# Last layer of a four-layer graph network: dots over halves of a turn, joined operations in the coefficients' chain, eight buffers of tails

## The reference

```
hyper_head = expmap0(head_emb)
hyper_tail = expmap(tail_emb, hyper_head)
hyper_rel = expmap(rel_emb, hyper_head)
res = project(mobius_add(hyper_tail, hyper_rel))
res = logmap(res, hyper_head) + ricci * 1e-07
res = jax.nn.relu(res)
sums = jnp.zeros((n_entities, res.shape[-1]), res.dtype).at[head].add(res)
...
return sums / jnp.clip(counts, 1.0, None)[:, None]
```

## Time and profile before

| | |
|---|---|
| time, median of 3 runs | 5223.61 us (5222.07 to 5224.58) |
| the profiled execution, first to last instruction | 6351.7 us |
| VectorE / GpSimd / TensorE / ScalarE busy in it | 3726.5 / 3463.1 / 2842.1 / 1728.7 us |
| mean granted TensorE clock | 0.618 |
| last layer in it | about 3205 us to the end |

### The profile page before, as it was taken

One profiled execution on the slowest core, in us unless ns is written; L12 is line 12 of the kernel. 1 busy time (PEld: TensorE's weight loads), 2 busy tenths in 40 slices (PEclk: granted clock), 3 DMA queues, 4 the chain that ended last, 5 costly groups with the idle time before them and its releaser, 6 DMA issues. The chain is left out here.

```text
span 6351.7 us, 75027 instructions
## 1 busy us (share of the span) xinstructions
PE 2842.1 (45%) x17919; PEld 2271.2 (36%) x17920; DVE 3726.5 (59%) x6870; ACT 1728.7 (27%) x5084; POOL 3463.1 (55%) x3375
## 2 busy tenths in 40 slices
PE   4544588433343334477614434434431343444442
PEld 1333456223333333345403333333331233333332
DVE  6444544255555666444426776667673767667678
ACT  0255200011111111000003354344340335445434
POOL 5667445466555663544265565566525556556551
PEclk7655699666666666678855555555555555555555
DMA  3720400355555554400021111111102111111110
GB/s 101 171 94 1 127 1 1 105 154 172 167 171 169 173 173 143 139 4 1 8 49 42 37 42 37 37 41 38 33 10 50 40 37 42 37 39 41 41 30 13
DMA packets 470914, 446.71 MB, mean 70 GB/s; under 512 B 113322, under 2 KB 417773, under 8 KB 470268
## 3 DMA queue, kind: packets, MB, share of 16 engines
q1 hardware_dynamic: 230602, 227.94, 12.4%
q0 software_dynamic: 116768, 136.51, 9.0%
q10 hardware_dynamic: 123282, 79.08, 4.5%
HBM read 306.93 MB, written 136.34 MB: 70 GB/s over the span
## 5 line engine op out<-in xcount | busy, mean ns | idle before, releaser
L2412 POOL DMA_INDIRECT tg<-tab_d,tail_ids x1632 | 1711.2, 1049 | 1191.1 <-DVEq L2731 644.9
L458 POOL DMA_INDIRECT sorted_edges_d<-place_batch x784 | 825.0, 1052 | 657.1 <-issue 220.6
L2437 PE MATMUL hr<-near_table,near_hot 128*128 x4896 | 654.4, 278 | 926.2 <-issue 593.1
L1598 POOL DMA_INDIRECT xg<-tab_d,src_i x784 | 768.0, 980 | 501.1 <-issue 241.6
L2445 PE MATMUL acc<-msg,sum_hot 128*96 128x65 f32 x3264 | 559.8, 364 | 902.1 <-ACT msg L2519 701.3
L2437 PEld LDWEIGHTS hr<-near_table,near_hot 128*128 128x128 f16 x4896 | 505.6, 108 | 1075.7 <-issue 970.2
L2445 PEld LDWEIGHTS acc<-msg,sum_hot 128*96 128x96 f32 x3264 | 536.4, 277 | 924.8 <-issue 924.7
L2492 ACT ACTIVATE pr<-hr 128x396 f32<-128x396 f32 x576 | 272.2, 482 | 1235.0 <-DMA b2col<-in_L_gnn_be_dram 786.9
L2513 ACT ACTIVATE pr<-pr,coef_c 128x64 f32<-128x64 f32 x1496 | 380.7, 340 | 82.4 <-issue 79.4
L2506 ACT ACTIVATE msg<-tg,coef_b 128x64 f32<-128x64 f32 x1632 | 399.1, 340 | 2.6 <-DVEq L2926 2.6
L2743 DVE TENSOR_REDUCE scal<-prod 128x17 f32<-128x1088 f32 x288 | 370.5, 1286 | 9.8
(11 more groups left out here) (504 smaller groups left out, 5392.9 us busy)
## 6 DMA issues: line engine op xcount, KB each, us to landing
ex<-spread_d SPq DMA_DIRECT2D x112, 448.0 KB
msg_d<-back ACTq DMA_DIRECT2D x112, 448.0 KB
near_hot<-head_row_d SPq DMA_DIRECT2D x96, 408.0 KB
tg<-tab_d,tail_ids POOLq DMA_INDIRECT x1632
spread_d<-zeros ACTq DMA_DIRECT2D x28, 896.0 KB
spread_d<-zeros SPq DMA_DIRECT2D x28, 896.0 KB
idsU<-dst_short_d SPq DMA_DIRECT2D x112, 224.0 KB
pairs_d<-pair_m SPq DMA_DIRECT2D x3, 4800.0 KB
```

The source lines that it names most:

```text
L458: l.eng.indirect_dma_start(K.sorted_edges[:, :], bass.IndirectOffsetOnAxis(ap=K.batch[:, n % 2, 0, k:k + 1], axis=0), K.batch[:, n % 2, 1, ...
L1598: l.eng.indirect_dma_start(xg[j.c % ROWS][:, half * H + k, :], None, K.tab1, bass.IndirectOffsetOnAxis(ap=src_i[:, t:t + 1], axis=0)).then ...
L2412: e.indirect_dma_start(tg[:, u % TAILS * GQ + k, :], None, K.tab3, bass.IndirectOffsetOnAxis(ap=K.tail_ids[:, u * GQ + k:u * GQ + k + 1], ...
L2437: ins = e.matmul(hr[(u * FILLS + g) % 2][:, c:c + PW3], near_hot[u % HOTS][:, k, :], rows[:, bass.ds(at[k] + n * PW3, PW3)], start=n == 0, ...
```

## The change

- `dot` works on halves of a turn: one product and one sum over 34 tiles (2176 elements per partition) for two over 17 each. It waits for both quarters of tails ahead of the product. `prod`, two tiles of a quarter, becomes one tile of two quarters.
- `TAILS` is 8, so that the tails of a turn lie next to each other (`T_`).
- In the chain, operations that stood side by side on neighbouring or evenly spaced rows of `sc` become one operation on two, three or four rows, partly with a broadcast. Rows are renumbered for it, and `kB`, `kC` become one tile `coef_bc`.
- Ten copies of lengths become three; the third, `PP`, is a packed copy of `PP_` (squared length of the head, read from `pr` with a stride), which the chain then reads.

```diff
-TAILS = 9
+TAILS = 8
...
-    prod = two("prod3", [P, GQ, D], F32)
+    prod = sb("prod3", [P, 2 * GQ, D], F32)
...
-            tt0(x[0], B, pt, MUL)
-            tt0(x[1], C, pr, MUL)
-            tt0(x[2], A, PP_, MUL)
+            tt0(terms[:, 0:3, :], abc, heads, MUL)
             tt0(x[3], C, tr, MUL)
-            tt0(x[4], B, q2[:, 0, :], MUL)
-            tt_(x[5], C, C, MUL)
+            tt_(terms[:, 4:6, :], abc[:, 1:3, :], q2, MUL)
...
-            def dot(n, x, y, quarters, taken=False, landed=False):
-                for q in quarters:
-                    u = now + q
+            def dot(n, x, y, halves, taken=False, landed=False):
+                for h in halves:
+                    at = slice(2 * h * GQ, (2 * h + 2) * GQ)
+                    u = now + 2 * h + 1
                     if taken:
                         v.wait_ge(near_taken, (u + 1) * FILLS)
                     if landed:
-                        v.wait_ge(got[u % TAILS], 16 * GQ * (u // TAILS + 1))
+                        for w in (u - 1, u):
+                            v.wait_ge(got[w % TAILS], 16 * GQ * (w // TAILS + 1))
                     v.wait_ge(l.sem, l.done())
-                    tt_(prod[q % 2][:, :, :], x(q), y(q), MUL)
+                    tt_(prod[:, :, :], x[:, at, 0:D], y[:, at, 0:D], MUL)
                     v.wait_ge(l.sem, l.done())
-                    v.tensor_reduce(sc[:, n, q * GQ:(q + 1) * GQ], prod[q % 2][:, :, :], AX.X, ADD).then_inc(l.sem, l.add(1))
-                    if q % 2 == 1:
-                        mark()
+                    v.tensor_reduce(sc[:, n, at], prod[:, :, :], AX.X, ADD).then_inc(l.sem, l.add(1))
+                    mark()
...
-            v.tensor_copy(q2[:, 1, :], R_[:, :, D])
-            for q in range(QN):
-                at = slice(q * GQ, (q + 1) * GQ)
-                v.tensor_copy(q2[:, 0, at], tg[:, tails(now + q), D])
-                v.tensor_copy(n2[:, 0, at], tg[:, tails(now + q), D + 1])
-            v.tensor_copy(n2[:, 1, :], R_[:, :, D + 1])
+            both_of = lambda x: x.rearrange("p k c -> p c k")
+            v.tensor_copy(sc[:, 2:25:22, :], both_of(T_[:, :, D:D + 2]))
+            v.tensor_copy(sc[:, 3:26:22, :], both_of(R_[:, :, D:D + 2]))
+            v.tensor_copy(PP, PP_)
...
-            for c in (cA, cB, cC):
-                tt_(c, c, A1(17), MUL)
+            tt_(abc, abc, three(A1(17)), MUL)
```

More of the change, by code:

```diff
@@ L2347, in edge_loop3 @@
     cA, cB, cC = (sc[:, n, :] for n in (26, 27, 28))
-    kB, kC = (two(n, [P, M], F32) for n in ("coef_b", "coef_c"))
-    terms = prod[0][:, :, :].rearrange("p k f -> p (k f)")[:, 0:9 * M].rearrange("p (n m) -> p n m", m=M)
+    coef_bc = two("coef_bc", [P, 2, M], F32)
+    kB, kC = ([c[:, n, :] for c in coef_bc] for n in range(2))
+    terms = prod[:, :, :].rearrange("p k f -> p (k f)")[:, 0:9 * M].rearrange("p (n m) -> p n m", m=M)
     zero = pr[1][:, 0:2, :].rearrange("p k f -> p (k f)")[:, 0:256].bitcast(F16)
@@ L2698, in vector, with form @@
         both = lambda x: x.unsqueeze(1).to_broadcast([P, 2, M])
-        def form(out, A, B, C, PP_, pt, pr, tr, q2):
+        def form(out, abc, heads, tr, q2):
+            A, B, C = (abc[:, n, :] for n in range(3))
             x = [terms[:, n, :] for n in range(9)]
-            tt0(x[0], B, pt, MUL)
-            tt0(x[1], C, pr, MUL)
-            tt0(x[2], A, PP_, MUL)
+            tt0(terms[:, 0:3, :], abc, heads, MUL)
             tt0(x[3], C, tr, MUL)
-            tt0(x[4], B, q2[:, 0, :], MUL)
-            tt_(x[5], C, C, MUL)
+            tt_(terms[:, 4:6, :], abc[:, 1:3, :], q2, MUL)
             l.eng.wait_ge(l.sem, l.done())
-            tt0(x[6], x[0], x[1], ADD)
+            tt0(x[6], x[1], x[2], ADD)
             st0(x[7], x[3], 2.0, x[4], MUL, ADD)
-            tt_(x[8], x[5], q2[:, 1, :], MUL)
+            tt_(x[8], x[5], C, MUL)
             l.eng.wait_ge(l.sem, l.done())
-            st0(x[0], x[6], 2.0, x[2], MUL, ADD)
+            st0(x[0], x[6], 2.0, x[0], MUL, ADD)
             tt_(x[1], B, x[7], MUL)
@@ L2738, in dot @@
                     if landed:
-                        v.wait_ge(got[u % TAILS], 16 * GQ * (u // TAILS + 1))
+                        for w in (u - 1, u):
+                            v.wait_ge(got[w % TAILS], 16 * GQ * (w // TAILS + 1))
                     v.wait_ge(l.sem, l.done())
-                    tt_(prod[q % 2][:, :, :], x(q), y(q), MUL)
+                    tt_(prod[:, :, :], x[:, at, 0:D], y[:, at, 0:D], MUL)
                     v.wait_ge(l.sem, l.done())
-                    v.tensor_reduce(sc[:, n, q * GQ:(q + 1) * GQ], prod[q % 2][:, :, :], AX.X, ADD).then_inc(l.sem, l.add(1))
-                    if q % 2 == 1:
-                        mark()
+                    v.tensor_reduce(sc[:, n, at], prod[:, :, :], AX.X, ADD).then_inc(l.sem, l.add(1))
+                    mark()
                 v.wait_ge(l.sem, l.done())
-            head = lambda q: P_[:, q * GQ:(q + 1) * GQ, 0:D]
-            kind = lambda q: R_[:, q * GQ:(q + 1) * GQ, 0:D]
-            tail = lambda q: tg[:, tails(now + q), 0:D]
+            T_ = tg[:, s * M:(s + 1) * M, :]
             def ask_scalar(k):
@@ L2756, in ask_scalar @@
                 v.wait_ge(answered, j * NA + k)
-            dot(dPR, head, kind, range(QN), taken=True)
-            dot(dPT, head, tail, range(2), landed=True)
-            dot(dTR, tail, kind, range(2))
+            dot(dPR, P_, R_, range(2), taken=True)
+            dot(dPT, P_, T_, range(1), landed=True)
+            dot(dTR, T_, R_, range(1))
             for q in range(QN):
@@ L2766, in vector @@
                     near(n + 1)
-            dot(dPT, head, tail, range(2, QN), landed=True)
-            dot(dTR, tail, kind, range(2, QN))
+            dot(dPT, P_, T_, range(1, 2), landed=True)
+            dot(dTR, T_, R_, range(1, 2))
             PT, PR, TR, d2 = A1(dPT), A1(dPR), A1(dTR), A2(dPT)
-            q2, n2, s2, t2, u2, a2, b2, X2 = A2(24), A2(2), A2(4), A2(6), A2(8), A2(10), A2(12), A2(14)
+            PP, heads, abc = A1(dPT - 1), sc[:, dPT - 1:dPT + 2, :], sc[:, 26:29, :]
+            q2, n2, s2, t2, u2, a2, b2, X2 = A2(2), A2(24), A2(4), A2(6), A2(8), A2(10), A2(12), A2(14)
             ask = A2(0)
             om = A1(23)
-            v.tensor_copy(q2[:, 1, :], R_[:, :, D])
-            for q in range(QN):
-                at = slice(q * GQ, (q + 1) * GQ)
-                v.tensor_copy(q2[:, 0, at], tg[:, tails(now + q), D])
-                v.tensor_copy(n2[:, 0, at], tg[:, tails(now + q), D + 1])
-            v.tensor_copy(n2[:, 1, :], R_[:, :, D + 1])
+            both_of = lambda x: x.rearrange("p k c -> p c k")
+            v.tensor_copy(sc[:, 2:25:22, :], both_of(T_[:, :, D:D + 2]))
+            v.tensor_copy(sc[:, 3:26:22, :], both_of(R_[:, :, D:D + 2]))
+            v.tensor_copy(PP, PP_)
             ts_(om, PP_, -1.0, 1.0, MUL, ADD)
@@ L2793, in vector @@
             tt0(a2, t2, u2, ADD)
-            tt_(X2, u2, both(PP_), MUL)
+            tt_(X2, u2, both(PP), MUL)
             l.eng.wait_ge(l.sem, l.done())
@@ L2803, in vector @@
             mark()
-            tt0(a2, a2, u2, MUL)
-            tt_(b2, b2, u2, MUL)
+            ab2 = sc[:, 10:14, :].rearrange("p (n two) m -> p n two m", two=2)
+            tt_(ab2, ab2, u2.unsqueeze(1).to_broadcast([P, 2, 2, M]), MUL)
             l.eng.wait_ge(l.sem, l.done())
             tt0(t2, b2, d2, MUL)
-            tt_(u2, a2, both(PP_), MUL)
+            tt_(u2, a2, both(PP), MUL)
             l.eng.wait_ge(l.sem, l.done())
@@ L2815, in vector @@
             tt_(s2, s2, q2, MUL)
-            tt0(A1(16), b2[:, 1, :], PR, MUL)
-            tt0(A1(17), a2[:, 1, :], PT, MUL)
-            tt_(A1(18), b2[:, 1, :], TR, MUL)
+            tt0(A2(16), both(b2[:, 1, :]), A2(dPR), MUL)
+            tt_(A1(18), a2[:, 1, :], PT, MUL)
             l.eng.wait_ge(l.sem, l.done())
             tt0(X2, t2, s2, ADD)
-            tt0(A1(16), A1(16), u2[:, 1, :], ADD)
-            tt_(A1(17), A1(17), A1(18), ADD)
+            tt_(A2(16), A2(16), sc[:, 9:19:9, :], ADD)
             l.eng.wait_ge(l.sem, l.done())
-            tt0(A1(16), A1(16), a2[:, 0, :], MUL)
-            tt0(A1(17), A1(17), b2[:, 0, :], MUL)
+            tt0(A2(16), A2(16), sc[:, 10:13:2, :], MUL)
             tt0(A1(18), X2[:, 0, :], X2[:, 1, :], MUL)
@@ L2841, in vector @@
             mark()
-            tt0(A1(6), A1(6), A1(18), MUL)
-            tt_(A1(7), A1(7), A1(18), MUL)
+            tt_(A2(6), A2(6), both(A1(18)), MUL)
             l.eng.wait_ge(l.sem, l.done())
[L2845 to L2848, removed]
+            tt_(sc[:, 25:29, :].rearrange("p (n two) m -> p n two m", two=2), A2(6).unsqueeze(1).to_broadcast([P, 2, 2, M]), ab2, MUL)
             l.eng.wait_ge(l.sem, l.done())
-            tt_(cA, A1(16), A1(17), ADD)
+            tt_(cA, A1(25), cA, ADD)
             l.eng.wait_ge(l.sem, l.done())
             yy = A1(29)
-            form(yy, cA, cB, cC, PP_, PT, PR, TR, q2)
```

(23 more changed lines are left out.)

## The result

The changed kernel takes 5354.02 us (5352.48 to 5355.92, 4 runs), the kernel before 5224.09 us beside it (4 runs): ratio 1.0246, 95% interval 1.0233 to 1.0259. It is 130 us slower, above the range of the prediction.

What follows compares the result with a forecast made beforehand. VectorE's order most likely set the last layer's turn, GpSimd just behind. Dots 2.6 plus chain 2.35 us over 24 turns gave 119, less 6 for first turns, 113, less 18 for late tails: -95, so 5129 us; range 5095 to 5290.

Steps and rivals of the forecast that it cites:

- The dots, 2.6 us per turn: VectorE's products and sums in the last layer: joining pairs takes 29.8 us per turn instead of 32.4, saving 2.6.
- the chain, 2.35: VectorE's small operations and copies: 22 fewer operations, three copies for ten and packed PP save 2.35 us per turn.
- 90.1 and 92.1 us per turn for VectorE and GpSimd: Last layer before the change: VectorE's own work 90.1 us per turn, GpSimd's 68 indirect DMAs 92.1.
- Blocking, 96.7 us per turn: GpSimd DMAs wait for joined products with two SBUF inputs: three pass per pair, GpSimd's turn becomes 96.7 us.
- rival 1: Last layer's turns: VectorE sets them, GpSimd mostly keeps up; -95 us, so 5129 us; chance 0.53, full or reduced.
- the 1128 us: Whole run: the profiled span of 6351.7 us exceeds the plain median by 1128 us, most waits belonging to that execution.
- rival 2: Joined products in the last layer: GpSimd becomes the bound, 6.6 us lost per turn; +89 us, 5313 us; chance 0.34.
- VectorE's 113 us: Last layer, 24 turns: 4.95 us per turn gives 119 us, less 6 for the hops' first turns, if VectorE sets the turn.
- GpSimd can run late by some 30 us before VectorE notices: Tail fetches in a plain run: a turn's last tails are asked for about 35 us before their product.
- the term of three free turns per hop (-30): GpSimd's slack in each hop: late by 11.5 us per turn, it lasts three turns, which still gain 5 each; -30.
- The last turn as the cleanest test, 84.7: Last turn of a hop, without standstills and with few DMAs: falls from 89.6 to about 84.7 us.
- No cost of eight buffers: Tail buffers: quarter u needs u-8 scaled, done in the turn's first 30 us, GpSimd asking then or later; cost nothing.

Runs made afterwards that it cites:

- base_look: The kernel before, unchanged, profiled again: 5233.64 us, profiled span 5231.9 us.
- one_input: Changed kernel with each joined product replaced by an equally long sum with one SBUF input, dots left out: 5166.83 us, ratio 0.9886.
- long_product: Changed kernel with one joined product, then two sums of a quarter each: 5359.82 us, ratio 1.0258.
- after_few_2: Changed kernel with 8 of 17 tail fetches per quarter left out once the ring is filled, second pair: 5134.50 us, ratio 0.9834.
- before_few_2: Kernel before, 8 of 17 tail fetches per quarter left out from the tenth quarter: 5219.99 us, ratio 0.9991; first run, `before_few`: 5838.41 us, ratio 0.9279.
- long_sum_2: Changed kernel with two quarter products back to back and one joined sum, second run: 5191.31 us, ratio 0.9937.

## Why the prediction was wrong

- **The dots, 2.6 us per turn, and the chain, 2.35**: right. 2420 and 2428 ns per joined operation; the ten copies' 0.93 us became 0.51 (3596.77 to 3597.28 us in the timeline of the changed kernel). Together 5.1 us measured for 4.95, where GpSimd does not set the turn. The rule of the Trainium skill that I weighed (VectorE: DVE Perf Modes, section on the TRN2 errata) gave 46 us more by an estimate; the chain with its copies saved 2.3 us of busy time per turn, as by the rows, where 3.5 by the rule would have been for the chain's operations alone.
- **90.1 and 92.1 us per turn for VectorE and GpSimd**: both 91.0. Right within 1.2%; VectorE by itself takes 90.8. That most waits of the earlier trace rows belong to that execution was right too: `base_look` has none above 1.1 us in the turn shown.
- **Blocking, 96.7 us per turn**: right to 0.2 us in the mean of a hop (1065.3 / 11 = 96.8), place and mechanism too (`one_input`, `long_product`). The prediction held back every DMA that begins up to 0.13 us ahead of a product, which is too many: one begun 0.03 us into it passes, one begun 0.07 us in is held. The sum does not change by it, since the third DMA of a pair begins 0.19 us ahead. The rule of the Trainium skill (SBUF - State Buffer, section Who interferes with whom) that two SBUF inputs contend with GpSimd's reads holds, for each operation by itself: the seam of two is enough. The same section infers that `tensor_tensor` does not stall DMAs, which the prediction left out; here it does, with 3.17 us for 0.94.
- **The failed step: rival 1 as the likeliest, with GpSimd as good as keeping up, since "the plain run issues DMAs faster than the profiled one".** It does not: 0.94 us and 0.30 between two, in a run of 5232 us as in one of 6352. What was shorter was the standstills of the other engines. I had put the 1128 us down to the profiling, and a lighter load for GpSimd with it; the constant 1.25 us in every row spoke against that, and I had noted it only in rival 2. GpSimd needs 96.9 us per turn after the change and sets it, so that none of VectorE's 113 us arrives and 130 are lost.
- **"GpSimd can run late by some 30 us before VectorE notices"**: wrong. The fetch ends 3.2 us ahead of its product in `base_look`, and the first ordinary turn of the changed kernel already takes 96.9 us: GpSimd has not rested since the hop's start, so there was no lead to use up. In rival 2 this made +89 us; the term of three free turns per hop (-30) does not exist, and the base is 91.0, not 90.1. Without that term the rival's own numbers give 5.7 us in each of 22 turns, 125 us (137 for 24), against 121.5 between the two spans: 5.5 per turn.
- **The last turn as the cleanest test, 84.7**: wrong for this kernel, 96.5. It waits 11.7 us for the tails of its own second half. VectorE's part of it was right: 84.6 in `after_few_2`, for 89.5 in `before_few_2`.
- **No cost of eight buffers**: right. 0.3 us gaps of GpSimd are ascribed to marks or to ScalarE for a few DMAs, none longer.

## What to carry to other kernels

When two engines tie, work out the second one's demand after the change from its own rows, and believe a duration that is the same in every stretch over an argument that plain runs must be faster. Where GpSimd issues DMAs all the time, keep each VectorE operation with two SBUF inputs short (here 1.29 us and not 2.42); those with one input (sums) could be lengthened without a loss (`long_sum_2`). Before a trace is used for sizes, its span should be near the plain time; if it is far off, waits in it may belong to that execution alone.

## Not expected of the hardware

- In the execution of the earlier trace rows, TensorE, ScalarE and at times VectorE stand still for up to 10 us with nothing in the profile that would have to release them, while GpSimd's DMAs stay at 1.25 us each. In `before_few`, with half of the fetches left out of the last layer, turns take 93.4 us where they took 117. What ties the two together is open.
- A DMA of GpSimd that waits for a VectorE product gets in between two products issued back to back, whose spans in the timeline overlap (two of 1.29 us in 2.50).
- The side that begins first has the way, and 0.04 us decide: a DMA begun 0.03 us into a joined product takes 0.94 us and stretches the product by 0.07, one begun 0.07 us in takes 3.17.
